# First attention of a decoder layer: scores, maxima and exponentials by pairs of key heads

## The reference

```python
B, T, E = (4, 512, 512)
H, KV = (16, 4)
G = H // KV
D = E // H
b, t, _ = x.shape            # 8, 256 here
scale = 1.0 / np.sqrt(D)
q = (x @ Wq).reshape(b, t, KV, G, D)
k = (x @ Wk).reshape(b, t, KV, D)
v = (x @ Wv).reshape(b, t, KV, D)
scores = jnp.einsum('bqhgd,bkhd->bhgqk', q, k) * scale
scores = jnp.where(causal_mask, scores, -jnp.inf)
w = jax.nn.softmax(scores, axis=-1)
y = jnp.einsum('bhgqk,bkhd->bqhgd', w, v)
return y.reshape(b, t, H * D) @ Wo
```

## The kernel before

| Engine | Order in a batch from the middle of the loop |
|---|---|
| PE | S0, VAL of b-1, S1, OUT of b-1, S2, Q0 and V of b+1, S3, K of b+1, two transposes of rows, Q1 of b+1 |
| DVE | M0, PB(3,1) of b-1, r, PB, r, OL, M1, PB(0,1), r(1,0), low part of x, PB(1,0), Res 0, r(1,1), M2, PB(1,1), r(2,0), Res 1, PB(2,0), norms, r(2,1), QL0, M3, PB(2,1), r(3,0), KL, PB(3,0), r(3,1) |
| ACT | E0, OH, high part of x, E1, E2, QH0, V, first half of E3, KH, second half of E3, QH1, features out |
| POOL | D of each unit in turn; RO between D(3,0) and D(3,1) |

## Time and profile before

### The profile page before, as it was taken

One profiled execution on the slowest core, in us unless ns is written; L12 is line 12 of the kernel. 1 busy time (PEld: TensorE's weight loads), 2 busy tenths in 40 slices (PEclk: granted clock), 3 DMA queues, 4 the chain that ended last, 5 costly groups with the idle time before them and its releaser, 6 DMA issues.

```text
span 1954.0 us, 36954 instructions
## 1 busy us (share of the span) xinstructions
PE 1810.4 (93%) x14704; PEld 1459.2 (75%) x14704; DVE 1156.2 (59%) x1812; ACT 643.0 (33%) x1380; POOL 266.2 (14%) x236
## 2 busy tenths in 40 slices
PE   4878886999995999999999999999999999999997
PEld 4767774788884777777878777777778787777775
DVE  4667664677765435565565564755645655646565
ACT  4545542212212324332242332423332322324331
POOL 1444443434331000000000000000000000000000
PEclk8889887899997999999999999999999999999999
DMA  4111120100002003030030020120300200300011
GB/s 148 50 47 51 43 68 17 56 12 21 11 0 87 7 11 79 14 101 13 7 88 11 7 91 6 36 61 13 81 11 12 84 13 6 91 6 13 7 49 43
DMA packets 49803, 76.92 MB, mean 39 GB/s; under 512 B 7873, under 2 KB 26433, under 8 KB 48961
## 3 DMA queue, kind: packets, MB, share of 16 engines
q1 hardware_dynamic: 49728, 75.88, 13.1%
HBM read 69.04 MB, written 6.82 MB: 39 GB/s over the span
## 4 chain that ended last, share of the span: by engine, by line
PE 58%; DVE 6%; issue 2%; ACT 1%; DVEq 0%; POOLq 0%; POOL 0%
PE pair L1811 10%; PE pair L1813 10%; PE pair L1812 10%; PE y_ps L1811 3%; PE y_ps L1813 3%; PE y_ps L1812 3%; PE pair L1933 2%; PE pair L1934 2%; PE qa_ps L1811 2%; PE qa_ps L1813 2%; PE qa_ps L1812 2%; PE qd_ps L1987 1%; PE qd_ps L1988 1%; PE qa_ps L1825 1%; PE qd_ps L1811 1%
## 5 line engine op out<-in xcount | busy, mean ns | idle before, releaser
L1811 PE MATMUL pair<-XH,GUH 128*128 128x512 f32 (+1 forms) x960 | 376.2, 392 | 0.0
L1813 PE MATMUL pair<-XH,GUL 128*128 128x512 f32 (+1 forms) x960 | 375.4, 391 | 0.0
L1812 PE MATMUL pair<-XL,GUH 128*128 128x512 f32 (+1 forms) x960 | 374.6, 390 | 0.0
L1725 DVE TENSOR_TENSOR h<-pair,sg 128x512 f32<-128x512 f32 (+1 forms) x120 | 82.8, 690 | 383.0 <-ACT sg L1497 382.9
L1497 ACT ACTIVATE sg<-pair 128x512 f32<-128x512 f32 (+1 forms) x120 | 71.6, 597 | 501.0 <-PE pair L1934 406.3
L1813 PEld LDWEIGHTS pair<-XH,GUL 128*128 128x128 f32 (+1 forms) x960 | 171.7, 179 | 47.8
L1812 PEld LDWEIGHTS pair<-XL,GUH 128*128 128x128 f32 (+1 forms) x960 | 171.9, 179 | 47.1
L1811 PEld LDWEIGHTS pair<-XH,GUH 128*128 128x128 f32 (+1 forms) x960 | 171.6, 179 | 47.0
L1399 POOL TENSOR_TENSOR qb_raw<-qb_raw,qb_scale 128x704 f32<-128x704 f32 x8 | 13.9, 1735 | 1043.2 <-DMA qb_scale<-in_gu_scale 1043.2
L366 ACT ACTIVATE p<-scores_ps,nm 128x128 f32<-128x128 f32 (+1 forms) x256 | 104.0, 432 | 102.7 <-DVE nm L451 102.7
L1547 DVE TENSOR_TENSOR HL<-h,HH 128x512 fp32r<-128x512 f32 (+1 forms) x120 | 83.0, 691 | 83.8 <-ACT HH L1409 83.8
(11 more groups left out here) (314 smaller groups left out, 3803.6 us busy)
## 6 DMA issues: line engine op xcount, KB each, us to landing
gu_raw<-in_gu SPq DMA_DIRECT2D x20, 512.0 KB, 4.1
wrep<-soft_f SPq DMA_DIRECT2D x64, 128.0 KB
dw_raw<-in_dw SPq DMA_DIRECT2D x10, 512.0 KB, 3.9
xT_raw<-in_xT SPq DMA_DIRECT2D x8, 512.0 KB, 4.1
x_raw<-in_x SPq DMA_DIRECT2D x8, 512.0 KB, 3.7
VR<-v_rows SPq DMA_DIRECT2D x32, 128.0 KB, 2.5
out<-xtok SPq DMA_DIRECT2D x4, 1024.0 KB, 4.2
gu_raw<-in_gu SPq DMA_DIRECT2D x10, 384.0 KB, 3.1
```

The lines of the kernel that those rows point to most:

```text
L1725: nc.vector.tensor_tensor(h[0:M, b, :], pair[b][1][0:M, :], sg[0:M, b, :], ALU.mult).then_inc(h_rdy, 1)
L1811: mm(out, wh, xh, start=first, stop=False)
L1812: mm(out, wh, xl, start=False, stop=False)
L1813: return mm(out, wl, xh, start=False, stop=last)
```

## The change

The heads are taken in two pairs. PE computes both tiles for heads 0 and 1 with the mask, signals, and then does the same for heads 2 and 3. DVE takes the maxima of a pair (two smaller reductions), ACT the exponentials of a pair (unit 0, then unit 1), and PE may overwrite a pair's banks as soon as that pair's exponentials are done. The counts of the semaphores follow: `s_done` counts two per group, `max_rdy` and `exp_done` four.

```diff
-            def exps(b, g, unit):
+            def exps(b, g):
                 u = g % 2
-                if unit == 0:
-                    after(act, pb_rdy, 2 * (G * b + g - 1))
-                    act.wait_ge(max_rdy, 2 * (G * b + g) + 2)
-                probs, keys = ((p0, P), (p1, S))[unit]
-                for kv in range(KV):
-                    n = 4 * unit + kv
-                    done = nc.scalar.activation(probs[:, u, kv, :], ...)
-                done.then_inc(exp_done, 1)
+                for pair in range(2):
+                    act.wait_ge(max_rdy, 4 * (G * b + g) + 2 * pair + 2)
+                    for unit, (probs, keys) in enumerate(((p0, P), (p1, S))):
+                        if pair == 0:
+                            after(act, pb_rdy, 2 * (G * b + g - 2) + unit + 1)
+                        for kv in (2 * pair, 2 * pair + 1):
+                            n = 4 * unit + kv
+                            done = nc.scalar.activation(probs[:, u, kv, :], ...)
+                        done.then_inc(exp_done, 1)
...
-                exps(b, 3, 0)
+                exps(b, 3)
                 if not last:
                     keys_high(b + 1)
-                exps(b, 3, 1)
...
             def maxima(b, g):
                 u = g % 2
-                for unit, keys in ((0, P), (1, S)):
-                    dve.wait_ge(s_done, G * b + g + 1)
-                    nc.vector.tensor_reduce(nm[:, u, 4 * unit:4 * unit + 4], s_ps[:, :, unit * S:unit * S + keys], AX_X,
-                                            ALU.max, negate=True).then_inc(max_rdy, 1)
+                for pair in range(2):
+                    heads = slice(2 * pair, 2 * pair + 2)
+                    dve.wait_ge(s_done, 2 * (G * b + g) + pair + 1)
+                    for unit, keys in ((0, P), (1, S)):
+                        nc.vector.tensor_reduce(nm[:, u, 4 * unit + 2 * pair:4 * unit + 2 * pair + 2],
+                                                s_ps[:, heads, unit * S:unit * S + keys], AX_X, ALU.max, negate=True).then_inc(max_rdy, 1)
 
             def reciprocals(b, g, unit):
                 u, n = g % 2, 4 * unit
-                dve.wait_ge(exp_done, 2 * (G * b + g) + unit + 1)
+                dve.wait_ge(exp_done, 4 * (G * b + g) + unit + 3)
...
             def scores(b, g):
                 pe.wait_ge(lo_rdy, NLO * b + (2 if g < 2 else 3))
-                after(pe, exp_done, 2 * (G * b + g))
-                alone(pe, past)
-                for n, (Q, K) in enumerate(((QH, KH), (QL, KH), (QH, KL))):
-                    for i in range(2):
-                        for kv in range(KV):
+                for pair in range(2):
+                    after(pe, exp_done, 4 * (G * b + g - 1) + 2 * pair + 2)
+                    alone(pe, past)
+                    for n, (Q, K) in enumerate(((QH, KH), (QL, KH), (QH, KL))):
+                        for i in range(2):
+                            for kv in (2 * pair, 2 * pair + 1):
```

More of the change, by code:

```diff
@@ L343, in queries_high @@
                 act.wait_ge(proj_done, NPJ * b + (1, 4)[w])
-                after(act, s_done, G * (b - 1) + (2, 4)[w])
+                after(act, s_done, 2 * G * (b - 1) + (4, 8)[w])
                 nc.scalar.activation(QH[:, 2 * w:2 * w + 2, :], y_ps[:, q_bank(b, w), :].rearrange("p (g s) -> p g s", g=2),
@@ L354, in keys_high @@
                 act.wait_ge(proj_done, NPJ * b + 3)
-                after(act, s_done, G * b)
+                after(act, s_done, 2 * G * b)
                 copy(KH[:], y_ps[:, k_bank(b), 0:S]).then_inc(hi_rdy, 1)
-            def exps(b, g, unit):
+            def exps(b, g):
                 u = g % 2
-                if unit == 0:
-                    after(act, pb_rdy, 2 * (G * b + g - 1))
-                    act.wait_ge(max_rdy, 2 * (G * b + g) + 2)
-                probs, keys = ((p0, P), (p1, S))[unit]
-                for kv in range(KV):
-                    n = 4 * unit + kv
-                    done = nc.scalar.activation(probs[:, u, kv, :], s_ps[:, kv, unit * S:unit * S + keys], ACT.Exp,
-                                                bias=nm[:, u, n:n + 1], accum_out=sums[:, u, n:n + 1])
-                done.then_inc(exp_done, 1)
+                for pair in range(2):
[5 more added lines that the diff above has]
+                            n = 4 * unit + kv
+                            done = nc.scalar.activation(probs[:, u, kv, :], s_ps[:, kv, unit * S:unit * S + keys], ACT.Exp,
+                                                        bias=nm[:, u, n:n + 1], accum_out=sums[:, u, n:n + 1])
+                        done.then_inc(exp_done, 1)
             def o_high(b, i, last):
@@ L394, in batch @@
             def batch(b, first, last):
-                exps(b, 0, 0)
-                exps(b, 0, 1)
+                exps(b, 0)
                 if not first:
@@ L402, in batch @@
                     weights_high(way.l_k, way.WKH, way.k_raw)
-                exps(b, 1, 0)
-                exps(b, 1, 1)
+                exps(b, 1)
                 if first:
                     weights_high(way.l_v, way.WVH, way.v_raw)
-                exps(b, 2, 0)
-                exps(b, 2, 1)
+                exps(b, 2)
                 if not last:
@@ L609, in scores @@
                 pe.wait_ge(lo_rdy, NLO * b + (2 if g < 2 else 3))
-                after(pe, exp_done, 2 * (G * b + g))
-                alone(pe, past)
-                for n, (Q, K) in enumerate(((QH, KH), (QL, KH), (QH, KL))):
-                    for i in range(2):
-                        for kv in range(KV):
[L616 to L622, removed]
+                for pair in range(2):
[4 more added lines that the diff above has]
+                            for kv in (2 * pair, 2 * pair + 1):
+                                rows = slice(HD * kv, HD * kv + HD)
+                                mm(s_ps[:, kv, i * S:(i + 1) * S], Q[rows, g, i * P:(i + 1) * P], K[rows, :],
+                                   start=n == 0 and i == 0, stop=False, skip_group_check=True)
+                    for kv in (2 * pair, 2 * pair + 1):
+                        done = mm(s_ps[:, kv, :].rearrange("p (c k) -> p c k", c=4)[:, 0:4:3, :], identR[:], tri[:],
+                                  start=False, stop=True, skip_group_check=True)
+                    done.then_inc(s_done, 1)
             def values(b, last):
```

## The result

The changed kernel takes 1966.61 us in the median of 11 runs (1962.33 to 1971.38), the kernel before 1957.28 in 11 (1953.53 to 1960.92). The ratio is 1.0047, with an interval of 1.0036 to 1.0058: it is 9.3 us slower, about half a per cent. The forecast was +2.0. The profiled execution has a span of 1966.2 us against 1954.0, so the 12.2 us between the profiles are somewhat more than those between the medians.

What follows compares the result with a forecast made beforehand. A loop of hand-overs, no single engine, bounds each batch. Later reciprocals +2.1, first batch -1.7 and half-clock scores +1.6 make +2.0 us on 1959.8: forecast 1961.8, own range 1953 to 1969, with rivals 1952 to 1971.

Steps and rivals of the forecast that it cites:

- The loop: First attention: hand-overs bound each batch, three times from maxima to unit 0's reciprocal, then divisions, row output, transpose, VAL.
- r of unit 0: Reciprocal of unit 0's sums on DVE: +0.10 us later at three places per batch, +2.1 us over seven batches.
- signs of being wrong: Group 3's or next group 0's maxima waiting for PE, D(3,1) waiting for r(3,1), or a batch under 34.0 or over 35.2 us.
- PE, the scores: Each group's scores on PE take 2.28 us instead of 1.38, +0.90; at full clock slack hides it, costing nothing.
- S1 at half clock: Group 1's scores behind two of seven VALs run at 1.2 GHz: +0.8 us each, +1.6 in all.
- KH behind E3: Copy KH moved behind group 3's exponentials on ACT: covered, no cost; 1 us to spare before D(3,1).
- The first batch: With no output work there, earlier exponentials bring group 1's unit 0 reciprocal forward, up to the first VAL: -1.7 us.
- The other signs: Profile after: full-clock batch 34.5 to 34.8 us, VAL's wait about 2.6, ACT's wait for maxima about 3 less per batch.
- Rival 1: PE becomes the bound between group 2's scores and group 3's maxima: slower, 1978 us; chance 12%.
- Rival 2: The loop runs over the end of the exponentials, through the scores: faster, 1941 us; chance 9%.
- Rival 3: A shorter wait before VAL keeps PE at full clock, up to 1 us per batch gained: 1953 us; chance 6%.

Runs made afterwards that it cites:

- experiment 3: The changed kernel with the exponentials of unit 0 of both pairs first, then unit 1: 1958.17 us, ratio 1.0006 to the kernel before.
- experiment 4: The changed kernel with scores four side by side as before and exponentials of unit 0 of both pairs first: 1952.03 us, ratio 0.9973.
- experiment 8: experiment 4 with two moves: on POOL the row output behind the last division, on DVE that division's transpose ahead of group 0's maxima: 1940.04 us, ratio 0.9906.
- experiment 2: The kernel before with only PE's scores in two masked pairs, one wait ahead and one signal behind: 1990.86 us, ratio 1.0169.
- experiment 5: The changed kernel with the scores of group 1 alone, those behind VAL, four side by side again: 1957.77 us, ratio 1.0009.
- experiment 10: The kernel before with the scores of group 1 alone two side by side with two masks: 1969.73 us, ratio 1.0060.
- experiment 1: The changed kernel with PE's scores four side by side as before, one mask and one signal; the rest by pairs: 1970.53 us, ratio 1.0070.
- experiment 9: The kernel before with the copy KH behind all eight exponentials of group 3 instead of between its two units: 1961.83 us, ratio 1.0018.
- experiment 12: The changed kernel with unit 0's exponentials first, group 1's scores four side by side, and the two moves of experiment 8: 1933.63 us, ratio 0.9880.

## Why the prediction was right or wrong

The time lies in the range (1952 to 1971), and the sign was that of the forecast. The size was not: +9.3 for +2.0. That the time lies in the range all the same is partly luck: the forecast of 1961.8 stands on a median of three runs, 1959.8, and with 11 runs the kernel before has 1957.28.

**The loop was read rightly.** VAL still waits for the transpose, D(3,1) still follows RO without a gap, r of unit 0 is what starts each step. Experiments 3 and 4 moved that reciprocal and the time followed; experiment 8 moved RO and M0 and VAL came sooner. One link was left out: PB(3,1) also stands behind M0 on DVE, and M0 waits for PE. Before, M0 ended at 168.96 and D(3,1) at 168.89, so a later S0 had no slack there. M0's second pair now waits 0.31 us for PE, one of the signs of being wrong that the prediction gave; it cost nothing here, since S0 starts earlier after r(3,0) (1.91 us for 2.22). In experiment 2, where M0 waits for both pairs, it cost 2 us a batch.

**PE, the scores: +0.90 predicted, +1.09 measured** (2.58 against 1.49, start of S2 to start of Q0). The prediction's 1.38 for a group before runs to 151.16, the start of a weight load; Q0's first matmul starts at 151.27. The twelve small matmuls of a pair take 0.91 us as computed. The two masks take 0.43 and not 0.235 where small matmuls follow (187.85 to 188.28), and 0.34 where matmuls of the whole array follow. So a change of the kind of tile costs about 0.1 us before the first matmul of the new kind and 0.1 between it and the next, each way; the prediction had counted one of the two halves for each change. That it was hidden at full clock was right: S3 starts without a wait, and M3 follows DVE's own work.

**r of unit 0: +0.10 three times predicted, +0.20 measured** (3.58 to 3.60 against 3.38). The first pair's maxima take 1.02 us as predicted, but ACT starts 0.12 us after them and not 0.04, and the six exponentials take 2.46 until r, not 2.4. In the batch of the rows above, with S1 at full clock, this term is the whole loss: 34.94 against 34.33 is 0.61 us, three times 0.20. Over seven batches it is 4 us, double what the sum had.

**S1 at half clock is the step that failed.** The prediction took the two S1 that lay at half clock before as given and priced the change at 0.8 us each, 1.6 in all. Of the 14.4 us that the seven batches lost in the profile, r of unit 0 makes about 4; the other 10 go with the 24 us more at half clock (78 for 54). Two things were missed.

The price. In the first batch S1 is at half clock in both kernels, and it takes 39.8 us for 36.0, of which r explains 0.6. The price is not the delay of S2 alone: the second pair's maxima wait 1.18 us for PE, and OUT starts later and runs at half clock too. Experiments 5 and 10 show this from both sides, -7.5 and +11.4 us for one group per batch, and the two batches compared in experiment 10 show it alone: 4.1 us up to S2 where four side by side lose 1.7. Whether the clock stays low longer because less of the array is in use or because the same work takes longer was not tested: the edit changes both.

The number. After the change there were four such S1 of seven. That is not the doing of S1's form: in each of the four the clock fell 6 to 8 us before S1 began, and with the scores four side by side throughout, experiments 1 and 8 have four and five such S1. Experiment 8 is the second fastest kernel here all the same. It goes in part with where the clock's fall lies against VAL: 14 times in the traces of all kernels here it fell in the last 0.6 us before VAL's start, and each time S1 met half clock, seven of them with four side by side. What moves the fall from kernel to kernel is open.

**KH behind E3** was covered, by the 0.3 us that KL ends before S0, for which the prediction had 0.2 (experiment 9).

**The first batch: -1.7 predicted.** From S0 to the first VAL it is 64.25 - 28.67 = 35.6 us after and 64.71 - 27.82 = 36.9 before: -1.3. The first VAL starts at 64.25 and not near 63.

**The other signs.** A batch with S1 at full clock took 34.94 us, a little over the 34.5 to 34.8 foreseen; those with S1 at half clock took far over the 35.2 that was given as a sign of being wrong. VAL's wait is 2.36 us for 2.6. ACT's wait for maxima fell by 1.4 us and not by 3.

**The rivals.** Rival 1 named the right engine and the right clock at the wrong place: PE does become late, between S1 and M2, and only where the clock is at half; at full clock it delays the second pair of M0 alone, by 0.31 us. Rival 2, the end of the exponentials, is refuted, since that came 0.7 us earlier after the maxima (5.2 us before, 4.5 after, in E2), S3 no longer waited, and nothing was gained. Rival 3, more full clock through the shorter wait in front of VAL, did not happen in the changed kernel; in experiment 12, with PE busy on both sides of VAL, it did behind three VALs, and gave a microsecond for each, as it was priced.

## What to carry to other kernels

When a group of instructions is split, look at which instruction the next engine waits for: here the fourth of eight exponentials became the sixth, which a new order of the same eight undoes. Small tiles that leave half of the array idle are cheap in time while PE waits anyway, but where they meet half clock they cost double and here kept it longer, so the same split can be harmless for three groups and bad for the fourth. And a term that hangs on the clock's state is not to be counted from the profile before: what the state costs changes with the edit, and how often it occurs changed in nearly every kernel here.

## What the runs showed of the hardware

- Two tiles of 32 rows side by side take as long as four: four matmuls in 0.24 us from start to start (187.28 to 187.52), where eight took 0.235. At half clock a pair with its masks takes 2.30 us instead of 1.34.
- Changing between tiles of 32 rows and the whole array costs about 0.2 us each way, half of it before the first matmul of the new kind and half between it and the next. Two masks take 0.43 us before small matmuls (187.85 to 188.28) and 0.34 before whole ones, where two in a row take 0.235.
- 288 matmuls of 32 by 32 take 6.6 us at half clock (142.75 to 149.36), 5.45 when the clock comes back within them after 3.5 us, and 4.5 us at full clock (experiment 12).
- An S1 that meets half clock puts S2 off by 1.7 us with four tiles side by side and by 4.1 with two, and the clock was at half for 10.2 and 13.7 us (experiment 10).
- Idle time that looks harmless can cost: with PE done sooner but waiting more, experiment 1 was no faster (1.0070) than the changed kernel (1.0047), and at half clock twice in a batch.
